# Maxima of the next groups three tiles earlier, shift rows through bank 7, context and key pieces five slots earlier

## What is computed

```python
q = _heads(xn @ q_w + q_b)                      # 16 batches x 256 rows, 16 heads of 8
kv = (context @ kv_w + kv_b).reshape(B, S, 2, H, HD)   # S = 1601
attn = jnp.einsum('bhnd,bhsd->bhns', q, k) * SCALE
attn = jax.nn.softmax(attn, axis=-1)
o = jnp.einsum('bhns,bhsd->bhnd', attn, v)
x = x + (o @ ca_proj_w + ca_proj_b)
```

## Time and profile before

| | us |
|---|---|
| median of 3 runs | 6270.36 |
| lowest and highest | 6269.71, 6271.52 |
| the profiled execution | 6276.06 |
| its span | 6274.1 |

### The profile page before, as it was taken

How to read it: one execution, slowest core, us unless ns; L and a number is a source line. 1 busy time by engine, 2 the same in 40 slices (tenths; PEclk the granted TensorE clock), 3 DMA queues, 4 the chain that set the end, 5 groups by cost and what they waited for, 6 DMA issues and landing times.

```text
span 6274.1 us, 225170 instructions
## 1 busy us (share of the span) xinstructions
PE 5577.9 (89%) x99544; PEld 3439.1 (55%) x99544; DVE 4131.0 (66%) x6523; ACT 4303.3 (69%) x8158; POOL 986.0 (16%) x1660
## 2 busy tenths in 40 slices
PE   5999999989878899999999878699999999998998
PEld 3555555555544455565556444355555555555665
DVE  5777777677555677777777355477777777754443
ACT  3777777777766688788887566467777777763333
POOL 3121121121111111111111011111221211200000
PEclk9999999999999999999999899899999999999999
DMA  2222212222112222222222011222222222211110
GB/s 89 83 67 65 85 57 75 73 61 79 42 57 66 86 74 69 75 86 77 77 67 76 11 59 57 70 61 85 69 63 85 67 65 85 65 52 32 46 57 26
DMA packets 230088, 414.17 MB, mean 66 GB/s; under 512 B 23904, under 2 KB 131472, under 8 KB 228624
## 3 DMA queue, kind: packets, MB, share of 16 engines
q1 hardware_dynamic: 229136, 400.04, 21.3%
HBM read 316.81 MB, written 83.14 MB: 64 GB/s over the span
## 4 chain that ended last, share of the span: by engine, by line
PE 63%; ACT 14%; DVE 10%; issue 4%; DMA 4%; POOL 3%; SPq 2%; DVEq 0%; ACTq 0%; POOLq 0%
PE bank L1087 23%; PE pair L1087 15%; PE bank L1195 12%; ACT P L1329 6%; DVE MX L1493 5%; ACT QP L1340 2%; DMA QP<-scr_q 2%; ACT REST L1300 2%; PE bank L700 2%; PE bank L691 1%; PE pair L627 1%; ACT KSF L1299 1%; PE pair L1182 1%; PE bank L1114 1%; DMA scr_ks<-KSF 1%
## 5 line engine op out<-in xcount | busy, mean ns | idle before, releaser
L1329 ACT ACTIVATE P<-bank 128x512 f32<-128x512 f32 (+1 forms) x5504 | 3185.4, 599 | 1080.0 <-PE bank L1087 1003.5
L1493 DVE TENSOR_REDUCE MX<-pair 128x2 f32<-128x802 f32 x3072 | 2927.6, 987 | 1088.5 <-PE pair L1087 1062.3
L1087 PE MATMUL bank<-QP,KP 128*32 128x256 bf16 (+2 forms) x40192 | 2167.9, 275 | 232.9 <-ACT P L1329 177.5
L1087 PE MATMUL pair<-KP,QP 96*32 96x401 bf16 (+2 forms) x25336 | 1801.3, 337 | 144.9 <-DMA QP<-scr_q 108.4
L1087 PEld LDWEIGHTS bank<-QP,KP 128*32 128x32 bf16 (+2 forms) x40192 | 1057.8, 96 | 1326.5 <-ACT P L1329 292.4
L1195 PE MATMUL bank<-P,VA 128*25 128x256 f32 (+1 forms) x22016 | 1739.1, 384 | 19.1 <-issue 18.6
L1087 PEld LDWEIGHTS pair<-KP,QP 96*32 96x32 bf16 (+1 forms) x25336 | 691.6, 97 | 347.3 <-DVE MX L1493 129.9
L1195 PEld LDWEIGHTS bank<-P,VA 128*25 128x25 f32 (+1 forms) x22016 | 625.7, 104 | 205.7 <-issue 76.9
L1497 DVE TENSOR_REDUCE MX<-pair 128x4 f32<-128x1024 f32 x256 | 311.3, 1222 | 332.3 <-PE pair L1087 331.5
L1618 POOL COPY VA<-VN 128x416 f32<-128x416 f32 (+1 forms) x320 | 140.7, 440 | 2360.8 <-PE bank L1195 2283.9
L1340 ACT CAST QP<-pair 2x512 bf16<-2x512 f32 x640 | 339.4, 576 | 144.1 <-PE pair L1182 132.2
(11 more groups left out here) (242 smaller groups left out, 4189.4 us busy)
## 6 DMA issues: line engine op xcount, KB each, us to landing
KP<-scr_k SPq DMA_DIRECT2D x768, 225.1 KB
QP<-scr_q SPq DMA_DIRECT2D x960, 48.0 KB
CN<-ctx_n SPq DMA_DIRECT2D x40, 768.0 KB
scr_k<-KSF SPq DMA_DIRECT2D x48, 600.8 KB, 3.2
scr_k<-KSF SPq DMA_DIRECT2D x48, 600.0 KB, 3.3
CT<-ctx_t SPq DMA_DIRECT2D x24, 800.5 KB, 4.5
KP<-scr_ks SPq DMA_DIRECT2D x128, 144.0 KB
scr_q<-QS SPq DMA_DIRECT2D x80, 192.0 KB, 2.1
```

The lines of the kernel that those rows point to most:

```text
L1087: last = nc.tensor.matmul(out[c:c + m, :], lhsT[:, c:c + m], rhs, start=start, stop=stop)
L1329: nc.scalar.activation(P[v % 2][0:kt, half * 2 * N:(half + 1) * 2 * N], SC[half][0:kt, :], ACT.Exp, scale=SCALE).then_inc(sem("probs_full" ...
L1493: nc.vector.tensor_reduce(MX[:, r, c:c + 2], MP[j % 2][:, :].rearrange("p (t k) -> p t k", t=2)[:, :, 0:SPANS[0][1]], AX.X, ALU.max).then_ ...
```

## The change

There are three parts, all in the order of the steps, with the same products and reductions.

1. **Maxima.** In cross phases the 16 maxima of a group are spread over 13 tiles, and these begin three tiles (`EARLY`) before the running group begins: tile `t` of a group makes the share `t + 3` of the next group, and its tiles 10, 11 and 12 make shares 0, 1 and 2 of the group after the next. Three of the 13 shares have two maxima (they fall in tiles 1, 5 and 10), the others one. The last maximum of the next group stands in tile 9. Before the first element of a cross phase, the four maxima of shares 0 to 2 of its second group are made too (`maxima_behind`).
2. **Shift rows.** In cross phases they are two pieces, `r0` and `r1` of each group, in tiles 11 and 12, four products and one copy each, into bank 7. On VectorE the bf16 part comes from a second reduction of `MX` and no longer from a cast of the first.
3. **Slots.** `stats0` to `stats12` go from slots 5 to 12 to slots 0 to 7, `ctx_scale` and `ctx_norm` from 12 to 8, `t0` from 18 to 14, `k0` from 20 to 16, `k3` from 28 to 23, `v0` from 36 to 34, `v3` from 45 to 42. `d` and `e` are made in strips.

SyncE's order is not changed.

```diff
-SHORT = ["mean", "var", "q", "k0", "k1", "k2", "k3", "y"]
+SHORT = ["mean", "var", "q", "k0", "k1", "k2", "k3", "d", "e", "y"]
...
+    def early(self, first, end):
+
+        return [j for j in range(self.nm) if first <= j * self.nt // self.nm < end]
+
     def prep_slots(self, host):
 
         if host.cross:
-            at = dict(mean=0, square=1, var=2, norm=2, q=6, v0=36)
+            at = dict(mean=0, square=1, var=2, norm=2, q=6, v0=34)
             if self.cross:
-                at.update({n: 5 + j * 8 // 13 for j, n in enumerate(STATS)})
-                at.update(ctx_scale=12, ctx_norm=12, t0=18, t1=19, k0=20, k1=22, t2=23, t3=24, k2=26, k3=28)
-                at.update(v1=38, v2=40, v3=45)
+                at.update({n: j * 8 // 13 for j, n in enumerate(STATS)})
+                at.update(ctx_scale=8, ctx_norm=8, t0=14, t1=15, k0=16, k1=18, t2=19, t3=20, k2=21, k3=23)
+                at.update(v1=36, v2=40, v3=42)
...
+            if ph.cross:
+                for g in range(NG if nxt else NG - 1):
+                    pieces += [(g * ph.nt + ph.nt - 2 + half, "rows", "r%d%d" % (g, half)) for half in range(2)]
...
+    def maxima(self, g, t):
+
+
+        ahead, far, nt = self.group(g + 1), self.group(g + 2), self.ph.nt
+        if not self.ph.cross or not ahead or not ahead[0].cross:
+            return [(*ahead, j) for j in ahead[0].maximum_at((t, nt))] if ahead else []
+        if t >= nt - EARLY:
+            p = t - (nt - EARLY)
+            return [(*far, j) for j in far[0].early(p, p + 1)] if far and far[0].cross else []
+        return [(*ahead, j) for j in ahead[0].early(t + EARLY, t + EARLY + 1)]
...
-                nc.vector.tensor_copy(NMB[g % 2][:, :, 0], NMF[:, :]).then_inc(sem("shift_step"), 1)
+                nc.vector.tensor_reduce(NMB[g % 2][:, :, 0], parts, AX.X, ALU.max, negate=True).then_inc(
+                    sem("shift_step"), 1)
```

More of the change, by code:

```diff
@@ L291, in build, with rows_before @@
         ph.misc_after = misc
+    rows_at, pairs = {}, 0
+    for ph in plan:
+        if isinstance(ph, Phase):
+            if ph.el["before"]:
+                rows_at[ph.name, 0, 0] = (None, pairs)
+                pairs += 2
+            for el in [ph.el["first"]] + [ph.el["middle"](i) for i in range(1, B - 1)] + [ph.el["last"]]:
+                for g in range(NG if el.nxt else NG - 1):
+                    t_ph, t_b, t_g = el.group(g + 1)
+                    if ph.cross:
+                        rows_at[t_ph.name, t_b, t_g] = (el.use("rows", "r%d0" % g), None)
+                    else:
+                        rows_at[t_ph.name, t_b, t_g] = (None, pairs)
+                        pairs += 2
+    def rows_before(ph, b, g):
+        if g or b:
+            return rows_at[(ph.name, b, g - 1) if g else (ph.name, b - 1, NG - 1)]
+        return rows_at[ph.before.name, B - 1, NG - 1] if ph.before else None
     stream_total = {k: (ph.misc_after, ph.after().get("stream_done", 0) if not isinstance(ph, LastPhase) else 0)
@@ L1093, in piece @@
                     return
+                use = el.use(role, name)
+                wait(pe, "misc_free", use)
+                if role == "rows":
+                    ph, b, g = el.group(int(name[1]) + 1)
+                    pe.wait_ge(sem("shift_ready"), ph.c.at("shift_ready", b, g + 1))
+                    for r in range(4):
+                        last = nc.tensor.matmul(MISC[MR:MR + 2, r * 128:(r + 1) * 128],
+                                                NMB[g % 2][:, 4 * int(name[2]) + r, :], IDB[:, :], start=True, stop=True)
+                    last.then_inc(sem("misc_full"), 1)
+                    return
                 ph, b = el.owner(role)
-                at, use = ph.c.at, el.use(role, name)
-                wait(pe, "misc_free", use)
+                at = ph.c.at
                 if name == "mean":
@@ L1214, in element @@
                         for j in js[:third]:
[L1215 removed]
+                            maximum(*j, first)
                         for piece_ in among:
@@ L1224, in element @@
                         for j in js[2 * third:]:
-                            maximum(*ahead, j, then)
-                        if ahead and t == ph.shift_tile:
+                            maximum(*j, then)
+                        if ahead and not ph.cross and t == ph.shift_tile:
                             shift_rows(*ahead)
                         for piece_ in behind:
-                            piece(el, *piece_)
+                            piece(el, *piece_, then if piece_[1] in SHORT else 128)
+                        for j in el.maxima_behind(g, t):
+                            maximum(*j)
             for ph in plan:
@@ L1240, in _ @@
                         shift_rows(ph, 0, 0)
+                        if ph.cross:
+                            for j in ph.early(0, EARLY):
+                                maximum(ph, 0, 1, j)
                     if ph is plan[0]:
@@ L1271, in piece @@
             def piece(el, role, name):
+                if role == "rows":
+                    g, half, use = el.group(int(name[1]) + 1)[2], int(name[2]), el.use(role, name)
+                    act.wait_ge(sem("misc_full"), use + 1)
+                    nc.scalar.copy(QP[g][MR:MR + 2, half * 2 * N:(half + 1) * 2 * N], MISC[MR:MR + 2, :]).then_inc(
+                        sem("misc_free"), 1)
+                    return
                 ph, b = el.owner(role)
```

46 lines of the change are left out of this document (29 added, 17 removed).

## The result

| | before | changed |
|---|---|---|
| median | 6270.94 (4 runs) | 6516.35 (4 runs) |
| lowest and highest | 6269.71, 6276.35 | 6510.29, 6516.99 |
| profiled execution, its span | 6276.06, 6274.1 | 6510.29, 6508.3 |

The changed kernel is slower: the ratio is 1.0387, with a 95% interval of 1.0369 to 1.0405. The prediction had the sign and the place of the loss. The loss is 245 us and not 104, and the time lies 51 us above the upper end of the range.

A forecast was written before the change was run, and what follows sets the result against it. TensorE bounds an element's last group, VectorE the first group in `a0` and `c2`. Terms of 185 - 96 - 8 + 8 + 15 = +104 us on 6276.06 made 6380; less 5.7, the forecast was 6374 us, range 6300 to 6465.

The forecast's parts named there:

- wait term: First groups of `a0` and `c2`: VectorE waits 7 to 8 us for the context before the statistics; +185 us.
- the clock: In 30 elements, a low clock window behind each new stall, mostly hidden by VectorE's backlog; +0.5 each, +15 us.
- maxima and rows: Groups that TensorE bounds: fewer tiles with two maxima and a changed group end save 0.6 us in 160 groups; -96 us.
- strips: Piece `d` in the 16 elements of `c1`: strips save 0.5 us each; -8 us.
- keys and values: New key and value slots: hardly matter, with the key packs' load hidden behind the running group.
- entries: Before the first element of each cross phase, four maxima made ahead cost 2.5 us, three times; +8 us.
- The wait for bank 7: Row pieces behind `k3` in slot 24: taken at nothing, at most 0.4 us in 48 groups.
- The rival with the full price: Each of 30 stalls costs up to 3.7 us by the low clock, up to 96 us more, 6470; chance 0.10.
- The stall isn't there: Context lands before VectorE asks, so the first group keeps 26.5 us and only gains remain; 6174 us, chance 0.06.
- Packing gives more: TensorE's idle time at group ends goes altogether, 240 us instead of 96; 6230 us, chance 0.04.

The follow-up runs named there:

- e3_early_load: Changed kernel with the next batch's context issued ahead of SyncE's wait for the last scores of group 3; 6245.41 us, ratio 0.9959.
- e9_part3_early: Kernel before with part 3's new slots and the early context load, without parts 1 and 2; 6356.69 us, ratio 1.0138.
- e6_both: Changed kernel with the early context load and each row copy of ScalarE between the two exponentials of its slot; 6197.16 us, ratio 0.9886.
- e10_de_wide: Changed kernel with early context load and row copies between the exponentials, but `d` and `e` in products of 128 columns; 6220.11 us, ratio 0.9915.
- e1b_parts12: Changed kernel with the old slots, part 3 undone, a row piece first where a slot has both; 6680.89 us, ratio 1.0659.
- e12_load_first: Changed kernel with the context issued behind SyncE's wait for group 3's scores, but ahead of that group's packs; 6325.2 us, ratio 1.0087.

## Why the prediction was wrong, step by step

The sum can be set beside the runs term by term, since the forecast put everything of the first groups of `a0` and `c2` into its wait term. Here all measured numbers are sums over groups and phases of the profiled executions, whose spans differ by 234 us.

| | forecast | measured | by |
|---|---|---|---|
| first groups of `a0` and `c2`, with the clock | +185 + 15 | +265 | changed kernel less before |
| maxima and rows, in the other groups | -96 | -53 | `e3_early_load` less `e9_part3_early`, without the strips |
| strips | -8 | -17 | `c1` of `e6_both` less `e10_de_wide` |
| keys and values in new slots, in the other groups | 0 | +22 | `e9_part3_early` less before |
| entries | +8 | +6 | changed kernel less before |
| `s1`, `s2` and what is left | 0 | +11 | |
| sum | +104 | +234 | |

So two terms failed by their size, the wait (65 us) and the maxima with their rows (43 us), and one step by its mechanism, the keys and values (22 us).

**The wait: the right mechanism, undersized.** VectorE's idle stretch, its cause, the pair that TensorE waits for and the group that pays came as told. Forecast were 33.2 and 32.1 us for the first group. It took 35.8 in the `a0` element shown (the median of the phase is 36.2) and 35.2 in `c2`. The term is a chain of three, and each link was short. The context was there at 10.1 us, not 9.7. From there to the shift it took 20.6 us (735.54 to 756.16), not 19.4; 0.88 of the difference is VectorE's wait for `RSTD`. The tail from the shift to the group's end was 5.0, not 4.1: VectorE reduces four maxima behind `y`, not two. These 2.6 us in `a0` (3.2 by the median) and 3.1 in `c2` used up the clock's 15 and made the 65 besides, less the one element of `a0` that didn't wait. I had added single instructions and left out what they wait for among each other.

**"Keys and values hardly matter": the step that failed by its mechanism.** It was one sentence, and wrong twice. First, their new slots cost time apart from the wait, about 1.0 us of an element by the medians: a value piece moved from a tile in which TensorE had idle time to one in which it had none. Summed over the phases it is 22 us, as the kernel before has some longer groups, among them the one with the window of the earlier trace rows. The prediction asked only when keys are needed, not what the new slots have beside them. Second, the keys' move is a condition of part 1, as `e1b_parts12` shows: without it the kernel is 6.6% slower than before, with TensorE waiting for the packs. I had "needed at slot 36 instead of 39" in the text and did not add up the way from the last key through its store and the packs' load to that slot.

**The maxima and rows: about half of the forecast.** Forecast was 0.6 us in each of 160 groups, and the groups that the term speaks of gave 0.33. `e3_early_load` less `e9_part3_early` is -111 us, which looks like the -96 with strips and entries. But 54 of it are in the first groups of `a0` and `c2` (28.5 to 26.8 and 28.0 to 25.6 us). There four maxima of the group are reduced in the element before, which shortens VectorE's backlog, and the prediction had counted this already, in its wait term ("eleven maxima"). That the two numbers lie close is luck. Most of the shortfall is the next step: with the copies moved (`e10_de_wide` less `e9_part3_early`) the same groups gave 0.50 each. In `c1` the third group gains 0.76 then and the fourth 0.69, as told, and the first and second 0.07 and 0.22. Those are full of pieces, and that this leaves few slots in which an exponential sets the pace is my reading. As the change has the copies, the third and fourth gain 0.65 and 0.52. A `c1` element was forecast at 85.4 us and took 87.1.

**"The wait for bank 7: nothing".** It was looked at for `k3`, and missed where the pieces follow each other: `r1` behind `r0`. It cost 38 to 48 us, which the order of two ScalarE instructions gives back.

**Strips and entries.** The strips were put at -8 and measured -23: -16.8 in `c1` by its phase's length; most of the rest shows in `s2` (6.3 us), for which I have no cause. The entries were put at +8 and are +6.2.

**The clock.** It fell in the wait, as told: 0.50 in the windows from 734 to 738, and the mean granted clock of the run went from 0.975 to 0.956. TensorE had stood still for 9 us before. Its price behind VectorE's backlog is what of it reaches VectorE, the 0.88 us for `RSTD`, so near the 0.5 that was put in and far from the 3.7 us of the earlier trace rows. Behind the wait, TensorE took 2.77 us (737.60 to 740.37) for a maximum, the products with `SQ` that `RSTD` needs, one half of scores and a product with the values. In the element of `e3_early_load` shown, at the full clock, the same four took 1.44. The view of waits has VectorE's waits for it, first in the changed kernel, then in `e3_early_load`:

```profile
DVE XN L1515 <- ACT RSTD L1355: 83.9, 47, 2.8
DVE XM L1515 <- ACT RSTD L1355: 31.3, 32, 2.2
```

```profile
DVE XN L1523 <- ACT RSTD L1363: 72.0, 34, 2.8
DVE XM L1523 <- ACT RSTD L1363: 19.3, 18, 2.2
```

That is 24 us more with the waits for the context than without, and so most of the 32 us that these cost beyond their own length. The rival with the full price did not happen, though its time of 6470 lies nearer to the result. The Trainium skill ("TensorE: Matmul & The Clock Gate", section "Loop structure matters more than you think") says that a wait for a DMA ahead of products makes them run cold. By that rule the trace agrees; what it costs here is smaller than the 1.3 us by which the four cold products were longer. That it is so because another engine has the backlog fits these rows, and no run shows it by itself.

**The other rivals.** "The stall isn't there" needed a landing earlier by 5 us. `e3_early_load` built that case but for one element: 6245, where the rival said 6174. The first groups of `a0` and `c2` cost next to nothing there (+8 us in all), as the rival had it; what it lacks is in the other groups, which gained 48 us and not 104. "Packing gives more" did not occur; even `e6_both` gains 72 us on the kernel before, not 240.

What stays open: why `s1` and `s2` are 5.1 and 3.1 us longer (`e12_load_first`, with the same three parts, has them only 0.7 and 0.0 longer), and where the last 8 us of the wait's price lie. Neither was tried.

The best version is `e6_both`, 6197 us, 1.1% faster than the kernel before: the change, with the context issued ahead of the wait for the scores and the row copies between the exponentials. It still has the late context in the first element of `c2`, whose first group takes 32.6 us against a median of 25.3.

## What to carry to other kernels

A consumer that moves ahead in a hand-made order needs its load moved ahead too: look in the issuing queue for a wait in front of that load, and take the landing time, not the issue, as the consumer's earliest start. For each moved piece ask both what its result must reach, link by link, and which engine has idle time in the slot that it leaves and in the one that it enters; a slot without work on the bottleneck engine is the cheapest place there is. When steps share one buffer, place what frees it (here a 0.58 us copy) ahead of anything else on its engine.

## What the runs showed of the hardware that I had not expected

A product with 8 moving columns in float32 costs 0.99 us as eight instructions of 128 columns and 0.28 as 32 strips of 32, 3.5 times less, with four times the instructions. Piece `e`, with 128 moving columns, only went from 1.08 to 0.87 (both by the start of the scores behind them). The Trainium skill ("TensorEngine Tiling (Array Packing)", section "Theoretical Speedup") gives up to four times for a small dimension. The trace has 3.5 times for `d`, and for `e` no more than 1.24.

TensorE's clock was at the lower level behind its wait of 9 us in the element shown, and yet removing the waits bought only little more than their own length: 80 us for 70, and 271 for 239.
